# Row blocks ahead of weights in two stage heads, zero fills spread over turns, and no `hold` in two edge stages

## What is computed

```
x = x + attention(layernorm(x), edge bias, Wq, Wk, Wv, Wo, src, dst)     # softmax over each node's edges
x = x + moe1(layernorm(x))     # H = gelu(x W1 + b1); gate = softmax(H Wg + bg); only the best of 8 experts, H Wd[e] + bd[e]
x = x + relational(layernorm(x), W of 8 relations, attn_src, attn_dst, edge type)   # softmax over each node's edges
x = x + moe2(layernorm(x))     # softmax router, best two of 8 experts, gelu(x w1[e] + b1) w2[e] + b2
```

## Time and profile before

| | |
|---|---|
| three runs, median (lowest to highest) | 5298.51 us (5294.61 to 5303.6) |
| profiled execution, its own time | 5326.32 us |
| its span | 5324.5 us |
| busy: TensorE, VectorE, ScalarE, POOL | 4280.5 (80%), 3132.7 (59%), 1838.4 (35%), 2166.5 (41%) |
| mean granted TensorE clock | 0.894 |
| HBM read, written | 423.60 MB, 115.55 MB |

### The profile page before, as it was taken

The page is one execution under the profiler, slowest core; times in us unless marked ns, Lnnn a source line. Parts: engine busy times, 40 slices in busy tenths (PEclk is TensorE's granted clock), DMA queues, the critical chain, the costliest instruction groups (busy, mean ns, idle before and its releaser), DMA issues. The chain is left out here.

```text
span 5324.5 us, 89607 instructions
## 1 busy us (share of the span) xinstructions
PE 4280.5 (80%) x21797; PEld 3214.9 (60%) x21798; DVE 3132.7 (59%) x8529; ACT 1838.4 (35%) x5242; POOL 2166.5 (41%) x2307
## 2 busy tenths in 40 slices
PE   7577777777776993799999577777777777999999
PEld 4355454544554993799644355555555556878877
DVE  5399999888996442011122166666666665555555
ACT  2244444444441330233233244333333422222222
POOL 4456666655661333000222366666665631111110
PEclk9799999999998995899999687788787888999999
DMA  6555655555552115111244333333333321000000
GB/s 190 162 153 169 169 168 164 161 162 163 167 169 94 39 40 186 55 35 37 104 178 175 127 92 93 90 91 92 91 93 89 94 61 42 16 14 14 16 14 11
DMA packets 231311, 543.03 MB, mean 102 GB/s; under 512 B 46241, under 2 KB 128686, under 8 KB 222158
## 3 DMA queue, kind: packets, MB, share of 16 engines
q0 software_dynamic: 112976, 348.83, 23.7%
q1 hardware_dynamic: 118013, 190.48, 10.3%
HBM read 423.60 MB, written 115.55 MB: 101 GB/s over the span
## 5 line engine op out<-in xcount | busy, mean ns | idle before, releaser
L277 POOL DMA_INDIRECT attn_KV<-kv_tab,attn_stage x832 | 866.5, 1042 | 560.6 <-issue 343.6
L1820 POOL DMA_INDIRECT rel_V<-h_tab,rel_stage x832 | 830.2, 998 | 570.8 <-issue 243.4
L392 PE MATMUL attn_SP<-attn_KV 128*128 128x264 f32 x1664 | 562.4, 433 | 263.5 <-DVE node L494 174.0
L1920 PE MATMUL rel_SP<-rel_V,rel_OH 128*128 128x264 f32 x1664 | 635.5, 505 | 170.8 <-DVE node L1991 134.7
L392 PEld LDWEIGHTS attn_SP<-attn_KV 128*128 128x128 f32 x1664 | 285.3, 200 | 482.7 <-issue 457.6
L379 PE MATMUL attn_QP<-node,attn_OHT 128*128 x1664 | 505.4, 431 | 45.0 <-issue 28.8
L1920 PEld LDWEIGHTS rel_SP<-rel_V,rel_OH 128*128 128x128 f32 x1664 | 350.0, 240 | 311.2 <-DVE node L1991 182.1
L1991 DVE TENSOR_TENSOR node<-node,rel_SP 128x264 f32 x832 | 351.4, 422 | 259.3 <-PE rel_SP L1920 140.4
L494 DVE SCALAR_TENSOR_TENSOR node<-node,same,attn_SP 128x264 f32 x832 | 397.4, 478 | 114.7 <-PE attn_SP L392 53.7
L2196 ACT ACTIVATE moe_HT<-moe_HB,moe_b 128x128 f32<-128x128 f32 x800 | 228.7, 368 | 670.0 <-PE moe_HB L2213 670.0
L2213 PE MATMUL moe_HB<-moe_YT,moe_W 128*128 128x128 f32 x3200 | 410.5, 283 | 0.0
(11 more groups left out here) (337 smaller groups left out, 6994.6 us busy)
## 6 DMA issues: line engine op xcount, KB each, us to landing
h_tab<-pr_H SPq DMA_DIRECT2D x50, 1056.0 KB
attn_KV<-kv_tab,attn_stage POOLq DMA_INDIRECT x832
rel_V<-h_tab,rel_stage POOLq DMA_INDIRECT x832
kv_tab<-qkv_KV SPq DMA_DIRECT2D x50, 256.0 KB
attn_runs<-runs SPq DMA_DIRECT2D x52, 192.0 KB
rel_runs<-runs SPq DMA_DIRECT2D x52, 192.0 KB
Wd<-in_wd SPq DMA_DIRECT2D x8, 1024.0 KB
y_sorted<-gate_zeros SPq DMA_DIRECT2D x8, 928.0 KB
```

The source lines that it names most:

```text
L277: pool.indirect_dma_start(out=KV[:, i * IT + u, 0:2 * FEAT], out_offset=None, in_=d["kv_tab"][:, :], in_offset=bass.IndirectOffsetOnAxis(a ...
L392: pe.matmul(SP[u % SUMS][:, 0:NUMC], KV[:, j * IT + u, 0:P], KV[:, j * IT + u, FEAT:ROW], start=True, stop=True).then_inc(s["sums"], 1)
L1820: pool.indirect_dma_start(out=V[:, i * IT + u, :], out_offset=None, in_=d["h_tab"][:, :], in_offset=bass.IndirectOffsetOnAxis(ap=stage[:, ...
L1920: pe.matmul(SP[(j + u) % SUMS][:, 0:NUMC], OH[:, j * IT + u, :], V[:, j * IT + u, :], start=True, stop=True).then_inc(s["sums"], 1)
```

## The change

Three things are changed.

1. In both edge stages `hold` is taken out in front of SP's loads, the gathers, `distances`, the sums of the first stage, and the column turns. The waits stay.
2. In the gate, SP issues X(0), then the weights (both halves of Wo first), and then goes on with X(1). The eight fills are issued in turns -2 to 3: one in each of four turns, then two in each of two. Wo has a semaphore of its own, `wo`, for which TensorE waits first; TensorE waits for the other five loads at turn 0, VectorE at turn 1; ScalarE waits for these five (LOADS is 5) where it waited for all.
3. In the top-2 stage SP issues X(0) and X(1), then the weights. They have three semaphores: TensorE waits for the router (`wr`) at turn -1, for `w1` and `w2` at turn 0, ScalarE for `w1` first, and VectorE for no weight.

```diff
@@ edge stages, the same cut in each place @@
                         need(sp, s["rows_f"], (k - RING + 1) * 3)
-                        hold(sp, m)
...
                                 need(pool, s["sums"], (k - RING) * IT + (u + 2))
-                                hold(pool, m)
...
                         need(act, s["masks"], k * QUADS + q)
-                        hold(act, m)
...
                             need(pe, s["added"], c * IT + (u + 1 - SUMS))
-                            hold(pe, m)
...
                         pe.wait_ge(s["row_sums"], 2 * g + 2)
-                        hold(pe, m)
@@ gate, SP @@
-        LOADS = 7
+        LOADS = 5
...
-                sp.wait_ge(s["zeroed"], 1)
...
+                def weights():
+                    for k in range(2):
+                        sp.dma_start(Wo[:, k, :], d["wo"][k * P:(k + 1) * P, :]).then_inc(s["wo"], 16)
+                    for k in range(2):
+                        sp.dma_start(W1[:, k, :], d["w1"][k * P:(k + 1) * P, :]).then_inc(s["w"], 16)
...
+                def fill(chunks):
+                    for k in chunks:
+                        sp.dma_start(flat[:, k * width:(k + 1) * width], zeros[:, :]).then_inc(s["filled"], 16)
...
                         slot_wait(sp, saved[i], t + 2, 16)
                         sp.sem_inc(s["y_saved"], 1)
+                    if isinstance(t, int) and t == -LEAD:
+                        weights()
+                    if isinstance(t, int) and t == -2:
+                        sp.wait_ge(s["zeroed"], 1)
+                    if isinstance(t, int) and -2 <= t < 2:
+                        fill([t + 2])
+                    if isinstance(t, int) and 2 <= t < 4:
+                        fill([2 * t, 2 * t + 1])
@@ gate, TensorE @@
-                pe.wait_ge(s["w"], 16 * LOADS)
+                pe.wait_ge(s["wo"], 32)
...
+                    if isinstance(t, int) and t == 0:
+                        pe.wait_ge(s["w"], 16 * LOADS)
@@ gate, VectorE @@
-                dve.wait_ge(s["w"], 16 * LOADS)
...
+                    if isinstance(t, int) and t == 1:
+                        dve.wait_ge(s["w"], 16 * LOADS)
@@ top-2 stage @@
+                    if isinstance(t, int) and t == 1 - LEAD:
+                        weights()
...
-                act.wait_ge(s["w"], 16 * LOADS)
+                act.wait_ge(s["w1"], 48)
...
-                pe.wait_ge(s["w"], 16 * LOADS)
...
+                    if isinstance(t, int) and t == -1:
+                        pe.wait_ge(s["wr"], 32)
+                    if isinstance(t, int) and t == 0:
+                        pe.wait_ge(s["w1"], 48)
+                        pe.wait_ge(s["w2"], 48)
...
-                dve.wait_ge(s["w"], 16 * LOADS)
```

More of the change, by code:

```diff
@@ L1095, in attend_and_route @@
     with ExitStack() as ctx:
-        s = sems(nc, m, "gate", "w zeroed filled clipped inverted o_ready o_turned oT attn_out x1 hidden gelu gated logits "
+        s = sems(nc, m, "gate", "wo w zeroed filled clipped inverted o_ready o_turned oT attn_out x1 hidden gelu gated logits "
                  "saved0 saved1 y_saved most shifted powed")
@@ L1126, in _ @@
             def _(sp):
-                for k in range(2):
-                    sp.dma_start(Wo[:, k, :], d["wo"][k * P:(k + 1) * P, :]).then_inc(s["w"], 16)
-                    sp.dma_start(W1[:, k, :], d["w1"][k * P:(k + 1) * P, :]).then_inc(s["w"], 16)
-                sp.dma_start(b1[:, :], d["b1"][:, :]).then_inc(s["w"], 16)
-                sp.dma_start(Wg[:, :, :].rearrange("p k e -> p (k e)"), d["wg"][:, :]).then_inc(s["w"], 16)
-                sp.dma_start(bg[:, :], d["bg"][0:1, :].to_broadcast([P, EXPERTS])).then_inc(s["w"], 16)
-                sp.wait_ge(s["zeroed"], 1)
                 flat = d["y_sorted"].rearrange("(p n) c -> p (n c)", p=P)
                 width = SORTED * FEAT // 8
-                for k in range(8):
-                    sp.dma_start(flat[:, k * width:(k + 1) * width], zeros[:, :]).then_inc(s["filled"], 16)
+                def weights():
[3 more added lines that the diff above has]
+                        sp.dma_start(W1[:, k, :], d["w1"][k * P:(k + 1) * P, :]).then_inc(s["w"], 16)
+                    sp.dma_start(b1[:, :], d["b1"][:, :]).then_inc(s["w"], 16)
+                    sp.dma_start(Wg[:, :, :].rearrange("p k e -> p (k e)"), d["wg"][:, :]).then_inc(s["w"], 16)
+                    sp.dma_start(bg[:, :], d["bg"][0:1, :].to_broadcast([P, EXPERTS])).then_inc(s["w"], 16)
+                def fill(chunks):
+                    for k in chunks:
+                        sp.dma_start(flat[:, k * width:(k + 1) * width], zeros[:, :]).then_inc(s["filled"], 16)
                 def body(t, i):
@@ L2116, in feed_forward_top2 @@
     with ExitStack() as ctx:
-        s = sems(nc, m, "moe", "w summed x3 based logits route powed c_turned cT bias_out hidden gelu experts mixed stored")
+        s = sems(nc, m, "moe", "wr w1 w2 summed x3 based logits route powed c_turned cT bias_out hidden gelu experts mixed stored")
         x_in = [new_sem(nc, m, f"moe_x_in{i}") for i in range(2)]
@@ L2142, in feed_forward_top2 @@
         node = lambda t, a=0, b=FEAT: m.node[:, bass.ds(t * NUMC + a, b - a)]
-        LOADS = 8
         LEAD = 7
@@ L2148, in _, with weights @@
             def _(sp):
-                for k in range(2):
-                    sp.dma_start(Wr[:, k, :], d["router"][k * P:(k + 1) * P, :]).then_inc(s["w"], 16)
-                    sp.dma_start(W1[:, k, :], d["m1"][k * P:(k + 1) * P, :]).then_inc(s["w"], 16)
-                    sp.dma_start(W2[:, k, :], d["m2"][k * P:(k + 1) * P, :]).then_inc(s["w"], 16)
-                sp.dma_start(b1[:, :], d["mb1"][:, :]).then_inc(s["w"], 16)
-                sp.dma_start(b2[:, :], d["mb2"][:, :]).then_inc(s["w"], 16)
+                def weights():
+                    for k in range(2):
+                        sp.dma_start(Wr[:, k, :], d["router"][k * P:(k + 1) * P, :]).then_inc(s["wr"], 16)
+                    for k in range(2):
+                        sp.dma_start(W1[:, k, :], d["m1"][k * P:(k + 1) * P, :]).then_inc(s["w1"], 16)
+                    sp.dma_start(b1[:, :], d["mb1"][:, :]).then_inc(s["w1"], 16)
+                    for k in range(2):
+                        sp.dma_start(W2[:, k, :], d["m2"][k * P:(k + 1) * P, :]).then_inc(s["w2"], 16)
+                    sp.dma_start(b2[:, :], d["mb2"][:, :]).then_inc(s["w2"], 16)
                 def body(t, i):
```

## The result

| | before | after |
|---|---|---|
| median (lowest to highest), 4 runs each | 5296.56 us (5278.11 to 5303.6) | 5173.43 us (5168.89 to 5176.14) |
| profiled execution, its span | 5326.32, 5324.5 | 5173.38, 5171.6 |
| mean granted TensorE clock | 0.894 | 0.909 |
| instructions | 89607 | 87630 |

What follows compares the result with a forecast made beforehand. VectorE and TensorE waiting for each other bound the edge stages, TensorE the gate, which loses only at its head. Terms -19.6 - 5.3 - 3.5 = -28.4 us took the 5298.5 us median to 5270 us; range 5244 to 5288.

Steps and rivals of the forecast that it cites:

- The gate's head: Start of the gate: with X(0) and Wo issued first, x1(0) starts 19.6 us earlier.
- the clock: Gate's head: an earlier restart may meet another phase of TensorE's half clock; 3 us either way, kept in the range.
- The fills: Gate: eight zero fills moved between X loads, costed at nothing; rival that they are not covered: 17.6 us, chance 0.09.
- The top-2 head: Start of the top-2 stage: X(0) and X(1) go before the weights, X(2) then binds; -5.3 us.
- The increments: Edge stages: removing `hold` saves 0.06 us at each of 59 real TensorE waits, -3.5 us; other engines nothing.
- POOL's, ScalarE's and SP's I cost at nothing: Edge stages: these engines' removed increments save nothing, as gathers run a period ahead and POOL itself waits.
- With that cover gone, 832 x 17 ns is 14 us: Edge stages: upper figure for POOL's removed increments if the gathers' lead and POOL's waiting did not hide them.
- TensorE's term: First edge stage: 59 sums that released VectorE, 0.06 us each, -3.5 us; ends nothing and 48 us.
- the increments do nothing: Rival, edge stages: where waits meet, one still needs its own instruction, so no saving; 5273 us, chance 0.14.
- Gathers lose their preparation: Rival, edge stages: a gather carrying its wait pays preparation again, 0.65 us a pair; slower, 5340 us, chance 0.03.
- What would have shown me wrong: Edge stages changing over 15 us, x1(1) lagging x1(0) by over 4.5 us, or the top-2 wait starting at X(1).

Runs made afterwards that it cites:

- e5: Changed kernel with an already met, non-incrementing wait added before every second gather of both edge stages: 5234.47 us, 0.9891 of before.
- e7: Kernel before with POOL's `hold` taken out only ahead of gathers 0, 12 and 14 of a period: 5336.18 us, 1.0080 of before.
- e8: Kernel before with POOL's `hold` taken out only ahead of gathers 2 to 10 of a period: 5173.77 us, 0.9774 of before.
- f3: Kernel before with SP's period loads of runs and bias cut to one partition and row from the fourth period, faster chip: 4865.43 us, 0.9999 of before.
- heads alone: Changed kernel with every `hold` of the edge stages put back, leaving the new stage heads and fills: 5279.01 us, 0.9962 of before.
- f4: Changed kernel with SP's period loads held back to the next period's second pair of sums, faster chip: 4847.16 us, 0.9958 of before.
- g4: Same kernel as f4, repeated on another chip of the faster kind: 4848.27 us, 0.9962 of before.

## Why the prediction was wrong

**The gate's head: right, a little short.** The term was -19.6; x1(0) came 18.3 us earlier relative to the last addition. The missing 1.3 us are Wo: TensorE's first transpose, which waits for it, starts 4.15 us behind SP's first issue and not 2.9. Of the 32 increments that the two halves of Wo send to its semaphore, 30 are there after 2.93 us, as forecast, and the last two after 3.29 and 4.11 us. In the ten traces with this head, of both kinds of chip, the last comes after 3.55 to 5.52 us, so the 2.0 us of a lone row block was too short for a wait that needs every increment of a pair of loads in a row of eight; what delays the last ones is not shown. x1(1) follows x1(0) after 3.81 us, so X(1) was early. Then the clock, kept in the range, took its share: the outputs of four turns ran at 2.07 us, half clock, and turn 0's hidden layer took 4.57 us, where before the fourth output was already at 1.13 and the hidden layer took 3.74. x1(4) is 17.35 us behind x1(0), not 15.42. 18.3 - 1.9 = 16.4, and the stage shows 15.7. Over all traces of the first kind the gate takes 348.2 us with the new head (3) and 367.1 without (7): -18.9.

**The fills: right.** They stand between X loads, four of them singly and then two pairs, VectorE has no wait for y_tab, and the gate's steady part is full. **The top-2 head: right.** Forecast -5.3, measured -5.4; X(2) is used 15.0 us after SP's first issue, forecast 14.5; the wait starts at X(2), 7.74 us and not some 10.

**The increments: wrong, and this is the whole miss.** The step that failed reads: "POOL's, ScalarE's and SP's I cost at nothing: the gathers run a period ahead". The reason is true and the conclusion isn't. Gathers of the first stage start some 20 us before VectorE uses their rows, in every kernel here, so no operation waited for a gather that was 0.75 us late. Yet POOL's part is 83 us. What the forecast had no term for is the stall of some 2 us, in which TensorE's increments come late and VectorE, ScalarE and POOL wait for them; VectorE's idleness falls from 2.60 to 1.76 us a period with POOL's `hold` out. That the phase of the gathers decides when it comes is argued from e5, e7, e8 and the counts; what holds the increments up is not shown. "With that cover gone, 832 x 17 ns is 14 us" named the wrong cover.
TensorE's term, 59 x 0.06 = 3.5 us with ends at 0 and 48, measured 29.5: inside its ends, but not by the mechanism, so that is luck. The load follows the addition by 0.05 us now only for the odd sums of a period (0.116 before); for the even ones it follows by 0.115, where it was 0.070. So the price of a wait nearly cancels over the two, and what shrank is the stall: VectorE's idleness fell by 0.5 us a period from before, most of it ahead of addition 12 (0.45 to 0.16 us) and little ahead of 14 (0.57 to 0.46). The count of 59 was itself thin: of 1551 such operations of TensorE in that stage of the trace of before, 775 have no semaphore event near their end, so who ended a wait is often not told; 103 additions stood behind more than 0.15 us of idleness. ScalarE's is nothing, as forecast. The sum of both terms on a chip without the stall is what the rival "the increments do nothing" said: the changed kernel gains 0.43%, forecast for that case 0.48%.

**The rival that was turned round.** "Gathers lose their preparation" put 0.65 us a pair on the side of a gather that carries its wait. The trace of before had the answer: a part of the "issue 343.6" in front of the gathers was the preparation behind a `hold`, not something a `hold` saves. The larger part is the 0.30 us that stand in front of any gather; 223.2 us are left in the changed kernel. And the profile of before did warn in another place. The group of VectorE's additions there:

```profile
L494 DVE SCALAR_TENSOR_TENSOR node<-node,same,attn_SP 128x264 f32 x832 | 397.4, 478 | 114.7 <-PE attn_SP L392 53.7 <-remote 46.9 <-DVE node L494 4.8
```

The forecast read the 53.7 us, 59 waits for a sum, and passed over the 46.9 us that no operation of the core explains. That is where a part of the stall shows in the group's row.

What would have shown me wrong was named (edge stages changing by more than 15 us), and it did.

## What to carry to other kernels

When many small instructions are taken out of a pipeline that waits on several engines, the sum over "real waits" prices only the waits; look also at idleness that the profile puts down to nothing on the core, find its place in the period, and count how often it is there. If it comes and goes with a shift of 0.1 us, as here, a price per instruction is no guide, and the honest range is as wide as the whole of that idleness, on both sides. Compare with more than one trace of the same program, since such idleness moved from place to place between two of them here. And measure on more than one chip before such a gain is booked: what a head or a queue order gives (15 to 20 us of 25 forecast) came everywhere, what the phases give came on one kind only.

## What was not expected of the hardware

*Two kinds of chip.* The kernel before takes 5294.0 and 5293.4 us on two chips and 4865.1, 4865.5 and 4866.8 on three, 8% less. Stages that are bound by TensorE take the same on both (the experts' stage 428 us); the edge stages take 1303 and 1132 (f3, whose small loads change nothing there) against 1471 and 1385 (heads alone).

*Increments that arrive late, in bursts.* On the faster kind, of 1551 operations of TensorE in the first edge stage that carry an increment (from VectorE's 31st product to its tenth from the end), 2 to 5 have no recorded semaphore event within 0.15 us of their end (23 and 31 in f4 and g4); on the slower, 650 to 792, and 31 to 47% of VectorE's and ScalarE's lack theirs too. The same program, the changed kernel, leaves 63,054 semaphore events on the one and 37,521 on the other. Most of them are landings of DMAs (41,929 and 20,221); the others are 21,125 and 17,300. So on the slower kind records are lost, and operations are late, in the same kernel. All runs of this study were recorded by the profiler, the timed ones too.
The Trainium skill ("NOTIFIC — the notification-queue block", Overflow: three behaviours, one of which stalls the engine) says that the block which writes such records holds its producers back rather than lose one inside. If that is what happens on the slower kind, removed increments and instructions help because they are fewer records to write, and the edge stages' gain would vanish without a profiler. No run here shows it, since all were recorded alike, and by itself it would not explain e7, which has fewer instructions and increments than before and is 43 us slower. That rival stays open.

*A gather's preparation.* Some 0.7 us in front of a gather can be done while it waits, if it carries the wait, and can't if an instruction ahead of it does (0.38 against 1.03 us of idleness). An instruction that only waits does the same as one that increments: 0.70 us from its end to the gather in e5, 0.73 in before.
